# Two reorderings of TensorE's instructions in a 16-head gated delta rule: chunk outputs ahead of a solve, and ahead of a masked level's products

## The reference

```python
x = x + layernorm(attn(layernorm(x), ...))
x = x + layernorm(ffn(layernorm(x), ...))
# attn, for each sequence and head:
q, k, v = split(silu(causal_conv4(x @ Wqkv))); z = x @ Wz
def step(M, inp):                      # over the tokens
    M  = M * exp(g_t)
    Mk = k_t @ M
    M  = M + outer(k_t, (v_t - Mk) * b_t)
    return M, q_t @ M
out = rmsnorm(out) * norm_w * silu(z)  # and then out @ Wout, summed over the heads
```

## Time and profile before

| what | value |
|---|---|
| median of 3 runs | 2787.56 us (2787.2 to 2790.44) |
| profiled execution, its time | 2786.65 us |
| its span in the trace | 2784.9 us |
| PE busy, matmuls | 2636.6 us, 95% |
| VectorE, ScalarE, GpSimd busy | 83%, 79%, 73% |
| mean granted TensorE clock | 0.981 of full speed |

### The profile page before, as it was taken

How to read it: one execution, slowest core, us unless ns; L and a number is a source line. 1 busy time by engine, 2 the same in 40 slices (tenths; PEclk the granted TensorE clock), 3 DMA queues, 4 the chain that set the end, 5 groups by cost and what they waited for, 6 DMA issues and landing times.

```text
span 2784.9 us, 70958 instructions
## 1 busy us (share of the span) xinstructions
PE 2636.6 (95%) x23924; PEld 2308.0 (83%) x23924; DVE 2305.1 (83%) x4996; ACT 2189.9 (79%) x7350; POOL 2023.3 (73%) x1802
## 2 busy tenths in 40 slices
PE   3399999999999999999999999999999999997898
PEld 2288888888888888888888888888888888885776
DVE  5588888888888888888888888888888888885683
ACT  2388888888888888888888888888888888873343
POOL 2267777877777787777777877777787777775553
PEclk9799999999999999999999999999999999997999
DMA  5322222222222222222222222222222223210110
GB/s 197 112 80 102 92 88 83 102 92 72 99 94 91 81 100 94 79 90 101 89 82 92 102 75 88 100 92 79 94 100 80 91 92 125 71 58 23 31 39 23
DMA packets 81011, 241.94 MB, mean 87 GB/s; under 512 B 8720, under 2 KB 23952, under 8 KB 64272
## 3 DMA queue, kind: packets, MB, share of 16 engines
q1 hardware_dynamic: 80656, 237.41, 24.4%
HBM read 223.75 MB, written 13.63 MB: 85 GB/s over the span
## 4 chain that ended last, share of the span: by engine, by line
PE 86%; DVE 4%; issue 2%; POOL 2%; ACT 1%; DMA 0%; SPq 0%; DVEq 0%; POOLq 0%; ACTq 0%
PE pj L1254 25%; PE pj L1402 9%; PE tr L1261 9%; PE g L1301 8%; PE st L1361 5%; PE op L1381 4%; PE op L1382 4%; PE st L1391 4%; PE st L1368 3%; PE bk L1320 2%; PE bk L1331 2%; PE bk L1334 2%; PE g L1425 2%; PE bk L1351 1%; PE g L1320 1%
## 5 line engine op out<-in xcount | busy, mean ns | idle before, releaser
L966 DVE SCALAR_TENSOR_TENSOR conv<-pj,cw,conv 128x511 f32<-128x511 f32 (+2 forms) x1152 | 847.5, 745 | 54.6 <-ACT conv L790 40.6
L1254 PE MATMUL pj<-xt,w_hi 128*128 128x512 f32 x2048 | 684.3, 415 | 17.3 <-ACT y L779 17.3
L644 POOL TENSOR_TENSOR kq<-kq,cum 128x512 f32<-128x512 f32 x256 | 442.0, 1747 | 0.0
L1254 PE MATMUL pj<-xt,w_lo 128*128 128x512 f32 x1024 | 404.0, 395 | 0.0
L1254 PEld LDWEIGHTS pj<-xt,w_hi 128*128 128x128 f32 x2048 | 348.4, 190 | 63.8 <-ACT y L779 17.7
L673 POOL TENSOR_TENSOR inv<-inv,x 128x512 f32<-128x512 f32 x128 | 148.3, 1159 | 340.0 <-ACT inv L849 340.0
L790 ACT ACTIVATE conv<-pj,cw 128x512 f32<-128x512 f32 x384 | 266.4, 694 | 123.3 <-PE pj L1254 113.3
L1043 DVE TENSOR_TENSOR y<-bk,mask 128x256 f16<-128x256 f32 x512 | 216.5, 423 | 163.7 <-PE bk L1320 157.3
L680 POOL TENSOR_TENSOR attn<-attn,part 128x512 f32<-128x512 f32 x256 | 326.6, 1276 | 0.0
L809 ACT ACTIVATE squares_out<-tr 128x128 bf16<-128x128 f32 x1024 | 273.7, 300 | 46.0 <-PE tr L1261 46.0
L1402 PE MATMUL pj<-wo,yt 128*128 128x256 f32 x1024 | 285.5, 401 | 0.8 <-DVE yt L1096 0.8
(11 more groups left out here) (201 smaller groups left out, 7877.8 us busy)
## 6 DMA issues: line engine op xcount, KB each, us to landing
xt<-xt_scratch SPq DMA_DIRECT2D x128, 1024.0 KB, 4.8
decay<-decay_scratch SPq DMA_DIRECT2D x128, 256.0 KB, 5.3
cum<-cumdecay_scratch SPq DMA_DIRECT2D x128, 256.0 KB, 5.6
w_raw<-in_w_heads SPq DMA_DIRECT2D x16, 512.0 KB, 7.0
xt_scratch<-xt_hi SPq DMA_DIRECT2D x8, 512.0 KB, 2.8
xt_scratch<-xt_lo SPq DMA_DIRECT2D x8, 512.0 KB, 3.8
x_in<-in_x SPq DMA_DIRECT2D x8, 512.0 KB, 4.2
out<-kq SPq DMA_DIRECT2D x16, 256.0 KB, 2.3
```

The costliest lines, as they stand in the source:

```text
L644: last = nc.gpsimd.tensor_tensor(part, part, of(cum, p)[:, :], ALU.mult)
L966: nc.vector.scalar_tensor_tensor(out=conv[:, i, j:SEQ], in0=pj[:, i % 2, 0:SEQ - j], scalar=cw[:, i, p // NSEQ, TAPS - 1 - j:TAPS - j], in ...
L1254: last = nc.tensor.matmul(pj[:, i % 2, :], w[:, kt, cols], x_[:, kt, :], start=(n == 0), stop=(n == 3 * KT - 1))
```

## The change

In TensorE's list of a step, `outputs(0, a - 3)`, with the wait `out_bank_free` ahead of it, now stands in front of `solve(1, a - 3)`, and `outputs(2, a - 3)` stands in front of `tx_level(2, a - 1)`. No instruction is added or removed, and no other engine's list changes.

```diff
@@ -1483,9 +1483,9 @@
                 from_state_k(1, a - 3)
                 z_level(4, a - 2)
                 turn_o(a - 4)
-                solve(1, a - 3)
                 out_bank_free(a - 3)
                 outputs(0, a - 3)
+                solve(1, a - 3)
                 tx_level(4, a - 2)
                 z_first(a - 1)
                 out_project(0, a - 4)
@@ -1505,8 +1505,8 @@
                 z_level(2, a - 1)
                 tx_level(6, a - 2)
                 outputs(1, a - 3)
+                outputs(2, a - 3)
                 tx_level(2, a - 1)
-                outputs(2, a - 3)
                 residual(a - 2)
                 state_update(2, a - 3)
                 turn_q(a)
```

## The result

| | before | changed |
|---|---|---|
| median of 5 runs | 2788.59 us | 2803.2 us (2801.54 to 2805.08) |
| profiled execution, span | 2784.9 us | 2800.8 us |
| VectorE's `gated` to `gated`, median of 111 steps | 18.70 us | 18.82 us |

The ratio is 1.0053 with a 95% interval of 1.0038 to 1.0067: slower by 0.5%, 14.6 us. The step is 0.12 us longer, and 125 full steps of it are 15 us. The difference is the same in every part of the loop.

A forecast was written before the change was run, and what follows sets the result against it. Two equally long loops bound the kernel: TensorE's own list, and `turn_q` through ScalarE, VectorE, `yt` and `out_project(0)`. -0.01 + 0.12 = +0.11 us a step, 125 times, is +13.8 us: 2801 us, range 2790 to 2808.

The forecast's parts named there:

- first move: `outputs(0)` ahead of `solve(1)`: fills its 0.19 us wait for `r`, but `out_project(0)` still waits for `yt`; -0.01 us a step.
- second move: `outputs(2)` ahead of level 2's products: its load then waits for `u` of chunk 2; +0.12 us a step.
- The idle gap before the load: Ahead of `out_project(0)` in the changed kernel: its load idles 0.1 us until `yt` is there.
- the slot of `out_project(0)`: In the kernel before, its load could undisturbed start at 1202.08 to 1202.10, just when `yt` arrives.
- `r`, the mask of level 4 and `yt` all come at a fixed time after `turn_q`: On VectorE: these results follow `turn_q` through ScalarE's and VectorE's gapless work, so `yt` does not move; load at 1202.10.
- VectorE does not wait for TensorE there: At `rhs(1)`, 1200.71 to 1201.05: VectorE's last listed wait is for ScalarE's V convolution, 27.0 us in 111 cases.
- the second of the two loops: `turn_q`, ScalarE, VectorE, `yt`, `out_project(0)`, rest of TensorE's list, `turn_q`: as long as TensorE's own list with its 0.19 wait.
- without an idle gap: VectorE from V's tap 1 to `gated`: claimed to work through with no wait for TensorE.
- The list alone counts: At `out_project(0)`: `yt` does not hold it, only TensorE's list matters; -0.07 us a step, 2779 us; chance 0.05.
- the load goes ahead: At `outputs(2)`: the weight load passes the wait for `u`, so no new wait; -0.07 us a step, 2779; chance 0.03.
- No change: Level 4's mask is the only new stop, or the `u` wait is 0.1 shorter; +0.02 a step, 2790; chance 0.07.
- Much slower: VectorE's run before `yt` lengthens in every step by 0.13 more; 0.24 us a step, 2817 us; chance 0.05.

The follow-up runs named there:

- the run with the other `u`: The changed kernel, but `outputs(2)` takes chunk 1's part of `u`, there long before, in place of chunk 2's: 2778.55 us, ratio 0.9968.
- the run with everything reordered: The kernel before with second move, `from_state_k(1)` and `solve(2)` inside projections, `solve(1)` ahead of `turn_o`, `state_update(1)` ahead of `out_project(0)`, `rhs(0)` and `q_norm` later: 2792.04 us, ratio 1.0011.

## Why the prediction was right

**Time and size.** Predicted 2801, range 2790 to 2808, with a step of 18.81; measured 2803.2 with 18.81 in the chain. The sum was right term by term: first move -0.01 (alone: 18.69 for 18.70, the last digit of the profile, and no difference in the times), second move +0.12 (alone: 18.82). On the times +13.8 us was predicted and +14.6 measured.

**First move.** `solve(1)` lost its wait, and `out_project(0)` took it over, at 0.05 to 0.06 behind `yt`. That the wait for `yt` eats the gain is shown by the run with `o` in its place, which gained 28.6 us. Two sizes were off. The idle gap before the load was put at 0.1 and is 0.19, since level 4's products and level 0 follow faster (1210.03 to 1210.26) than in the old order (0.31). It did not change the sum, as `yt` was the later one anyway. And the slot of `out_project(0)` was put at 1202.08 to 1202.10; the wait was already 0.03 in the kernel before.

**Why `yt` stands where it does.** Here the prediction's step was incomplete: "`r`, the mask of level 4 and `yt` all come at a fixed time after `turn_q`", "VectorE does not wait for TensorE there". The run with VectorE's list shortened shows that VectorE cannot start `rhs(1)` before `from_state_k(1)` is done; in the kernel before this has no line in the list of waits, as VectorE's own work ends within 0.04 us of it. So the second of the two loops is not the long one through `turn_q` and ScalarE alone; the stretch from `from_state_k(1)` to `out_project(0)` has the same length. And "without an idle gap" hid the 0.85 us in which `rhs(0)` or `q_norm` is stretched beside GpSimd. For this change both readings give the same number, since neither `turn_q` nor `from_state_k(1)` is moved against `out_project(0)`; that the incomplete one did no harm was luck. For anyone who wants the gain they differ: the first says "shorten VectorE's run", which gave nothing.

**Second move.** `outputs(2)` waited for `u` of chunk 2, at the load, with 0.42 in the chain; with another `u` the loss was gone. The trace agrees with the load standing behind the wait, not pulled ahead of it: the load goes 0.05 after `u` ends, though its weights were there long before. By the rule of the Trainium skill (TensorE: Matmul & The Clock Gate, "Step-by-step: what each phase is for"), taken to reach past a waiting matmul, the change would have gained 0.07 us a step. That the later place of level 2's products costs nothing was right too: with the products of level 2 where the change puts them, the run with the other `u` was 0.3% faster than before. Only the list of waits was to show some 20 us here and shows no line.

**The rivals.** "The list alone counts" (2779) fell with the first move alone; "the load goes ahead" (2779) with the changed trace. "No change" (2790) fell with a step of 18.82 where it needed 18.72: the wait for `u` had its full size. "Much slower" by a longer VectorE run did not come.

## What to carry to other kernels

When a full engine waits at one place for another engine, look for the next place in its list that waits for a later result of the same engine. Filling the first wait with other work only moves it to the second place, as long as the work between the cause and the second place, in the waiting engine's own list, stays the same. What gains is more work between the cause (`turn_o`) and that place (`out_project(0)`). Here one pair was moved in between, in a run in which the other inputs of VectorE's run had been made ready earlier, and the whole gained 0.8%.

An instruction that starts without an idle gap can be held from two sides at once, by its own queue and by its input. If cutting one side gains nothing, the other holds it; that costs one run.

## What was not expected of the hardware

- A group of two float32 matmuls takes 0.30 us in the chain behind float16 work and 0.22 behind float32 work, also in other places than the earlier trace rows: `solve(1)` 0.30 in the run with everything reordered, 0.22 elsewhere when it does not wait. `state_update(2)` behind `residual` (float16) takes 0.28. A pair behind float32 work that takes more than 0.22 was found waiting: `state_update` at 1216.68 in the kernel before takes 0.30 behind L1382, and its load goes at 1216.50, 0.05 after ScalarE's `u` ends at 1216.45, with no line in the waits. One such change of type less was worth 0.07 us a step in the run with the other `u`, with no wait involved.
- VectorE starts 0.11 us after the chain's end of `from_state_k` but 0.04 after that of the transposes (`turn_o`, 1217.08 to 1217.12). A handover that looks slack by 0.07 us need not be; why the two differ was not tried.
- A wait at a weight load may be on no line of the waits and still cost 0.12 us in the chain (0.42 for 0.30), and 0.20 against the same place without it: the load idles only 0.13 us, but without a wait loads start ahead of their matmuls' turn in the chain, in the earlier trace rows at 1201.32 for L1382, whose piece starts at 1201.60.
